# A graph layer's pair loop: three groups of matmuls take other places in TensorE's order

## The reference

```
xn = layernorm(x)
# graph: 16 relations, 100000 edges sorted by dst
transformed = einsum('ni,rio->rno', xn, weight)
gnn = segment_sum(transformed[rel_type, src] * norm, dst)
# attention without a mask, in heads of 32, and a gate
context = einsum('bnhd,bnhv->bhdv', softmax(k, axis=1), v)
out = einsum('bnhd,bhdv->bnhv', q, context)
gate = sigmoid(gelu(ln(xn) @ Wg1 + bg1) @ Wg2 + bg2)
x = x + gnn + out * gate @ Wproj + bproj
# 8 experts, each row takes the best two
t = layernorm(x)
rw, re = top_k(softmax(t @ router_w.T), 2)        # rw divided by its sum
x = x + t + sum_e combine[:, e] * (gelu(t @ w1[e] + b1[e]) @ w2[e] + b2[e])
```

## Time and profile before

| | |
|---|---|
| median of three runs | 1621.45 us |
| profiled execution, its own time | 1623.3 us |
| its span | 1621.6 us |
| mean granted TensorE clock | 0.992 of 2.4 GHz |
| TensorE busy over the span | 97% |
| VectorE busy | 83% |
| GpSimd busy | 64% |
| ScalarE busy | 60% |

### The profile page before, as it was taken

How to read it: one execution, slowest core, us unless ns; L and a number is a source line. 1 busy time by engine, 2 the same in 40 slices (tenths; PEclk the granted TensorE clock), 3 DMA queues, 4 the chain that set the end, 5 groups by cost and what they waited for, 6 DMA issues and landing times.

```text
span 1621.6 us, 31747 instructions
## 1 busy us (share of the span) xinstructions
PE 1579.1 (97%) x10509; PEld 1442.6 (89%) x10509; DVE 1346.7 (83%) x3391; ACT 965.5 (60%) x2156; POOL 1030.0 (64%) x1109
## 2 busy tenths in 40 slices
PE   6899999999999999998699999999999999999998
PEld 5788888888888888887699999999999999999998
DVE  7878665488888888874699999999999999999985
ACT  4454222255655655553677766777667777677764
POOL 3443322577777777746777777777777777777720
PEclk9999999999999999999899999999999999999999
DMA  8677665688899888878433333343333333333320
GB/s 264 204 262 259 240 259 225 214 289 281 272 287 295 273 283 285 285 249 299 143 110 117 101 100 111 105 118 99 101 112 103 117 102 102 112 104 114 105 58 10
DMA packets 127076, 290.50 MB, mean 179 GB/s; under 512 B 21271, under 2 KB 49724, under 8 KB 126914
## 3 DMA queue, kind: packets, MB, share of 16 engines
q1 hardware_dynamic: 86068, 177.19, 29.8%
q0 software_dynamic: 39952, 110.13, 25.8%
q10 hardware_dynamic: 894, 1.16, 0.2%
HBM read 149.49 MB, written 138.90 MB: 178 GB/s over the span
## 4 chain that ended last, share of the span: by engine, by line
PE 68%; DVE 18%; issue 6%; ACT 3%; POOL 3%; DMA 1%; DVEq 0%; ACTq 0%; POOLq 0%
PE bank L1767 54%; DVE ml L1552 3%; DVE xres L1682 3%; DVE ht L1668 2%; POOL raw L685 2%; PE bank L1970 2%; PE bank L1811 2%; PE bank L1812 2%; DVE sel L1536 2%; PE bank L1971 2%; PE bank L1822 1%; PE bank L1922 1%; ACT mh L1010 1%; ACT raw L1066 1%; PE bank L1966 1%
## 5 line engine op out<-in xcount | busy, mean ns | idle before, releaser
L799 POOL DMA_INDIRECT stg<-table,idxcur x495 | 560.0, 1131 | 215.8 <-issue 114.7
L1767 PE MATMUL bank<-wreg,xt 128*128 128x512 f32 x2352 | 583.3, 399 | 4.9 <-DVE wreg L1151 2.3
L1767 PEld LDWEIGHTS bank<-wreg,xt 128*128 128x128 f32 x2352 | 436.6, 190 | 94.2 <-DVE wreg L1151 2.5
L685 POOL DMA_INDIRECT raw<-table,idxa x297 | 304.6, 1026 | 87.7 <-issue 75.6
L1767 PE MATMUL bank<-tt,wreg 128*128 128x256 f32 (+1 forms) x2400 | 318.6, 282 | 2.2 <-DVE tt L1618 2.2
L1767 PE MATMUL bank<-wreg,ht 128*128 128x256 f32 x2352 | 313.1, 282 | 0.2 <-DVE ht L1668 0.2
L1767 PEld LDWEIGHTS bank<-tt,wreg 128*128 128x128 f32 x2400 | 295.8, 189 | 5.4 <-issue 2.6
L1767 PEld LDWEIGHTS bank<-wreg,ht 128*128 128x128 f32 x2352 | 291.3, 188 | 0.4 <-DVE ht L1668 0.4
L1066 ACT ACTIVATE raw<-bank,cols 128x256 f32<-128x256 f32 (+1 forms) x400 | 165.0, 464 | 96.9 <-PE bank L1767 96.9
L1193 DVE COPY stg<-bank 128x512 f32<-128x512 f32 x196 | 133.6, 686 | 97.2 <-PE bank L1767 96.5
L1552 DVE SCALAR_TENSOR_TENSOR ml<-stg,nrm,mh 128x256 fp32r<-128x256 f32 x455 | 195.7, 480 | 16.0 <-ACT mh L1010 15.7
(11 more groups left out here) (244 smaller groups left out, 2136.8 us busy)
## 6 DMA issues: line engine op xcount, KB each, us to landing
table<-stg SPq DMA_DIRECT2D x196, 512.0 KB, 3.7
kv_d<-kvs SPq DMA_DIRECT2D x49, 256.5 KB, 5.2
xt_d<-xt SPq DMA_DIRECT2D x49, 256.0 KB, 4.6
xtp<-xt_d SPq DMA_DIRECT2D x24, 512.0 KB
stg<-table,idxcur POOLq DMA_INDIRECT x495, 2.9
sk<-kv_d SPq DMA_DIRECT2D x24, 256.5 KB, 5.7
out_x<-xres SPq DMA_DIRECT2D x24, 256.0 KB
xres<-in_x POOLq DMA_DIRECT2D x23, 256.0 KB, 4.5
```

Source lines behind the costliest of these rows:

```text
L685: pool.indirect_dma_start(ring_a[:, r * EARLY + j, :], None, table[0:LIMIT, :], bass.IndirectOffsetOnAxis(ap=idxa[:, at:at + 1], axis=0)). ...
L799: pool.indirect_dma_start(stg[:, (s % 4) * SUP + j, :], None, table, bass.IndirectOffsetOnAxis(ap=idxcur[:, at:at + 1], axis=0)).then_inc( ...
L1767: mm = pe.matmul(dst, stat(a, c), mov(b, c), start=(n == 0), stop=(n == 3 * chunks - 1))
```

## The change

Three entries change their place in the table, and one argument lets `*SUMS` name its slot. Only TensorE has functions for the entries that move, so the other engines keep their order, word for word.

```diff
 SLOTS_OF_PAIR = (
-    ("-WEIGHT", ..., "-LAYER1 2", "-LAYER2 0", "*SUMS", "+OUT", "+GATES"),
+    ("-WEIGHT", ..., "-LAYER1 2", "-LAYER2 0", "+OUT", "*SUMS", "+GATES"),
     ...
-    ("-ADD 1", ..., "-LAYER1 4", "-LAYER2 2", "*SUMS", "+PROJ", "-COMBT"),
-    ("-ADD 2", ..., "*MSGS", "+STATS", "-LAYER1 5", "-LAYER2 3", "*SUMS"),
-    ("-ADD 3", ..., "-LAYER1 6", "+NORM", "-LAYER2 4", "*SUMS"),
-    ("-ADD 4", ..., "-LAYER1 7", "+TURN", "+TURN_HI", "-LAYER2 5", "*SUMS",
+    ("-ADD 1", ..., "-LAYER1 4", "-LAYER2 2", "*SUMS", "-COMBT"),
+    ("-ADD 2", ..., "*MSGS", "+STATS", "-LAYER1 5", "+PROJ", "-LAYER2 3", "*SUMS"),
+    ("-ADD 3", ..., "-LAYER1 6", "+NORM", "-LAYER2 4"),
+    ("-ADD 4", ..., "-LAYER1 7", "*SUMS 4", "+TURN", "+TURN_HI", "-LAYER2 5", "*SUMS",
      "-BIAS2"),
 ...
             if groups:
-                steps[name](i, s, groups)
+                steps[name](i, *map(int, expert or (s,)), groups)
```

More of the change, by code:

```diff
@@ L2108 @@
 SLOTS_OF_PAIR = (
-    ("-WEIGHT", "*SELECT", "-LOW 1", "*MSGS", "*WINDOW", "-COMB", "-COMB_HI", "-LAYER1 2", "-LAYER2 0", "*SUMS", "+OUT",
+    ("-WEIGHT", "*SELECT", "-LOW 1", "*MSGS", "*WINDOW", "-COMB", "-COMB_HI", "-LAYER1 2", "-LAYER2 0", "+OUT", "*SUMS",
      "+GATES"),
     ("-COMB_LOW", "*SELECT", "-ADD 0", "-LOW 2", "*MSGS", "+GATE_ACT", "+GATE", "-LAYER1 3", "-LAYER2 1", "+GATE_HI", "*SUMS"),
[L2112 to L2116, removed]
+    ("-ADD 1", "*SELECT", "-LOW 3", "*MSGS", "+GATE_LOW", "*WINDOW", "-LAYER1 4", "-LAYER2 2", "*SUMS", "-COMBT"),
+    ("-ADD 2", "*SELECT", "-LOW 4", "-COMBT_ACT", "*MSGS", "+STATS", "-LAYER1 5", "+PROJ", "-LAYER2 3", "*SUMS"),
+    ("-ADD 3", "*SELECT", "-LOW 5", "*MSGS", "+MEAN", "*WINDOW", "-LAYER1 6", "+NORM", "-LAYER2 4"),
+    ("-ADD 4", "*SELECT", "-LOW 6", "*MSGS", "*LAST_WINDOW", "-LAYER1 7", "*SUMS 4", "+TURN", "+TURN_HI", "-LAYER2 5", "*SUMS",
      "-BIAS2"),
```

## The result

| | before | after |
|---|---|---|
| median of the runs | 1623.11 us (4 runs, 1619.91 to 1625.02) | 1606.55 us (4 runs, 1604.45 to 1609.29) |
| profiled execution, its own time | 1623.3 us | 1606.8 us |
| its span | 1621.6 us | 1605.0 us |

The changed kernel is faster: ratio 0.9901, 95% interval 0.9877 to 0.9925. The forecast of 1610.3 us was 3.8 us too high, inside the forecast's own range of 1605 to 1616. In a second comparison (experiment 5, five runs beside 27 of the kernel before) the ratio was 0.9911, 0.9892 to 0.9930.

A forecast was written before the change was run, and what follows sets the result against it. A pass was taken as a loop through VectorE, TensorE's stalls mostly slack: 0.41 us a pass, 23 times, is 9.4, with 1.8 in pass 1 11.2, so 1612.1 us profiled and a 1610.3 us median; range 1605 to 1616.

The forecast's parts named there:

- The wait of slot 3: VectorE's wait for ScalarE's high halves in slot 3: gone with COMBT earlier, 0.27 us a pass (bounds 0 and 0.27).
- The add of expert 5: VectorE's 0.35 us wait on TensorE in slot 5 goes; 0.21 returns as TURN_LOW's wait for ScalarE, leaving 0.14 a pass.
- OUT in regular passes: OUT ahead of slot 0's sums saves TensorE 0.32 us, alone worth nothing in a regular pass; cover for the projection.
- Pass 1: OUT fills TensorE's idle time ahead of slot 0's sums, GATES come 2.3 us earlier; gain 1.8 us (bounds 0 and 2.5).
- the half clock: Granted clock 0.50 from 773.4 to 780.0 us; GATES and short sums falling into it lose some 0.5 us.
- The sum over a pass: A regular pass gains 0.27 + 0.14 = 0.41 us, to 33.20; 9.4 us over 23 passes.
- Rival A: TensorE sets the pace and all its stalls, 0.89 us a pass, come back: 1599.1 us; chance 0.11.
- Rival B: Roots take over slot 3's 0.27 us, TURN_HI the add's 0.35; only the first pass gains: 1619.6 us; chance 0.17.
- the wait that the prediction had named as a sign of being wrong: MEAN on VectorE waiting for GpSimd's roots would show the prediction wrong; no size was given.
- Rival C: Slower: STATS waits for the later projection, a pass 0.3 us longer, 1626.6 us; chance 0.06.
- the cover: Margin by which the moved projection ends before VectorE's STATS needs it: 0.3 us, or 0.05 without the gain on TensorE.
- The prediction is wrong if the pass falls below 32.9: A regular pass under 32.9 us would mean VectorE's loop with ScalarE is not what holds it.

The follow-up runs named there:

- experiment 5: The changed kernel again, unaltered, beside the kernel before on a chip like the first: 1608.45 us, ratio 0.9911.
- experiments 2 and 9: The kernel before with the projection alone moved behind the first product of expert 5, on slower chips: 1719.59 us, ratio 0.9975, and 1719.09 us, ratio 0.9936.
- 3 and 10: The kernel before with slot 4's sums alone moved behind the first product of expert 7, on slower chips: 1711.08 us, ratio 0.9952, and 1712.27 us, ratio 0.9904.
- experiment 1: The kernel before with OUT alone put ahead of the sums of slot 0, on a slower chip: 1691.44 us, ratio 0.9825.
- experiment 6: The kernel before, with GpSimd's first gather of slot 3 waiting for the end of VectorE's COMB: 1620.90 us, ratio 0.9982.
- experiment 7: The changed kernel, with GpSimd's first gather of slot 3 waiting for the end of COMB: 1616.63 us, ratio 0.9959 to the kernel before.
- experiment 11: The changed kernel with passes 0 and 1 in the old order, on a slower chip: 1692.25 us, ratio 0.9789 to the kernel before.
- 12: The changed kernel with NORM's second half in slot 6 and LAYER2 5 ahead of slot 4's sums, on a slower chip: 1704.05 us, ratio 0.9854 to the kernel before.
- experiment 4: The changed kernel with passes 0 and 1 in the old order, on a slower chip: 1692.18 us, ratio 0.9817 to the kernel before.

## Why the prediction was right, and what it missed

- **The wait of slot 3, 0.27: right.** Gone in the changed kernel and in experiments 2 and 9, unchanged in 3 and 10.
- **The add of expert 5, 0.14: right.** 0.35 went and 0.19 came back ahead of TURN_LOW, so 0.16.
- **OUT in regular passes, nothing: nearly right.** Its 0.32 on TensorE took nothing off the two waits above (experiment 1). But it took a wait off the add of expert 1, 0.02 a pass in the kernel before and 0.10 once COMB is quick (experiment 6); the prediction had overlooked that add. The worth in time was not measured.
- **Pass 1, 1.8: 1.45, near by luck.** Two things that the sum had wrong nearly made up for each other. I expected GATES and the sums in the half clock, and a gate 1.8 us earlier; the row shows the full clock from 773 to 780, and the gate came 3.30 earlier. The Trainium skill, "TensorE: Matmul & The Clock Gate", Part 1, has activity as what releases the throttle, and here the trace agrees: OUT filled the idle time. Then the roots, for which the sum charged nothing, gave 1.15 back in pass 1 and 0.70 in pass 2, where GpSimd came to them behind its gathers.
- **The sum over a pass, 0.41 forecast, 0.67 measured: the term that was missing is COMB.** The sum took VectorE's durations as fixed and only its waits as movable. But 16 of 22 passes had 0.36 us of hold-up inside COMB, written as busy time. (16 - 3) / 22 x 0.36 = 0.21 a pass, and 0.27 + 0.16 + 0.21 + 0.02 = 0.66 of the 0.67. By itself COMB's share is 22 x 0.21 = 4.6 us, most of the 5.3 by which the forecast for the profiled execution missed (1612.1 against 1606.8).
- The Trainium skill, "SBUF — State Buffer", SBUF: two separate sides, says that VectorE and GpSimd share a pair of ports under an exclusive lock, held for a whole instruction, and that on VectorE's side only some operations take it (those that use both ports, or have two inputs in SBUF). That fits the long L1639s, which end with the gather, and experiment 6; it doesn't fit L1636 and L1638, which run to their end inside the gather, nor the 71 quick L1639s: the same instruction is held up at one point of a gather and not at others. No run here tells a port from another shared thing.
- **Rival A, TensorE sets the pace: no.** It had the shares for it, and has them more than ever: 724.02 of 724.38 us busy over the regular passes, its weight loads 717.38, VectorE 681.97. In experiment 7 a wait of VectorE's alone made the pass longer by 0.61 where 0.62 was its price. By the rule of the Trainium skill, "Perfetto Trace Analysis", Identifying the Most-Contended Engine, TensorE was the engine to work on; the trace doesn't agree here.
- **Rival B, waits that change names:** half of the add's did (0.19). The roots took over in passes 1 and 2, the wait that the prediction had named as a sign of being wrong; from pass 3 on MEAN never waits in the two traces of the changed kernel, but the margin is small. On a slower chip (experiment 11) it waited in nine passes, and holding GpSimd's gathers until COMB's end made the roots the bound at once.
- **Rival C, STATS behind the projection:** never in a regular pass of the changed kernel. There the cover is 0.27 (0.3 forecast): the projection's last matmul would release STATS near 1115.28, and it starts at 1115.55. Where the cover was gone (a few passes of experiments 2 and 12) the wait showed.
- "The prediction is wrong if the pass falls below 32.9" was drawn too near: it fell to 32.93 between TURN_LOWs (32.96 between COMBTs), through VectorE's loop and not past it.

## What to carry to other kernels

Between two engines that are both nearly full, find which one's waits move the distance of two passes one for one; shares of busy time and the chain of waits named TensorE here and were wrong about it. Look at the spread of one line's durations before taking them as fixed: here a median of 392 ns beside a shortest of 145 was a hidden wait. And measure a shift at an instruction that the change has not itself moved.

## What the runs showed of the hardware

**A GpSimd gather can hold up VectorE's tiny operations** by 0.36 us in a chain of eight (0.97 to 1.33), the last of those inside it ending with the gather; it does so only where that one starts 0.53 to 0.55 us into the gather, and not at 0 to 0.47. Of two executions of the same changed kernel one had 3 such passes of 22 and the other 7, with passes of 32.96 and 33.03 us.

**Chips differ by 6% on this program, and in kind.** On the two slower ones the first sum of pass 0 comes some 50 us later and a pass takes 33.9 to 35.6 us. There ScalarE hears late of matmuls that are recorded as done. In the changed kernel's first trace, LAYER1 0 on TensorE and the gelu that waits for it on ScalarE:

```profile
1126.24 1.70 PE L1767 MATMUL bank<-tt,wreg 128*128 128x256 f32 x12
```
```profile
1127.97 0.84 ACT L1066 ACTIVATE raw<-bank,cols 128x256 f32<-128x256 f32 x2 [1.30 <-PE bank L1767]
```

The gelu starts 0.03 after the product's end (1127.94). The same pair in experiment 4:

```profile
1098.55 1.69 PE L1767 MATMUL bank<-tt,wreg 128*128 128x256 f32 x12
```
```profile
1102.33 0.84 ACT L1066 ACTIVATE raw<-bank,cols 128x256 f32<-128x256 f32 x2 [3.35 <-remote]
```

Here it is 2.09 us (1100.24 to 1102.33); ScalarE has such a wait in 21 passes, and its releaser has no name. The place depends on TensorE's order: with slot 4's sums moved it was the same on both slower chips (passes of 34.81 and 34.84 us), with the projection moved it was another. Since the ends of matmuls are modelled, TensorE may really stand still there; on what, the records don't show, and it stays open. It may be why OUT's move alone brought 28 us on such a chip; that is not shown, for the kernel before has no trace there.
